# Five banks for the turned scores and one for the output in a narrow cross-attention

## The reference, cut to what matters

```python
query = (layernorm(x) @ w_q.T)                  # 128 queries, 32 heads of 16, 8 groups of 4 heads
key, value = ctx @ w_k.T, ctx @ w_v.T           # 2048 keys, 8 heads of 16, one for each group
scores = einsum('bghnd,bgsd->bghns', query, key) / 16 ** 0.5
scores = where(mask, scores, finfo.min)
attention = softmax(scores, axis=-1)
x = x + einsum('bghns,bgsd->bghnd', attention, value) @ w_out.T
```

## Time and profile before

| | us |
|---|---|
| median of 3 runs (1639.43 to 1639.99) | 1639.66 |
| profiled execution, device time | 1641.53 |
| profiled execution, span from first to last instruction | 1639.7 |
| PE (TensorE matmul) busy | 1529.1 (93%) |
| DVE (VectorE) busy | 1018.2 (62%) |
| ACT (ScalarE) busy | 874.7 (53%) |
| POOL (GpSimd) busy | 401.8 (25%) |

### The profile page before, as it was taken

How to read it: one execution, slowest core, us unless ns; L and a number is a source line. 1 busy time by engine, 2 the same in 40 slices (tenths; PEclk the granted TensorE clock), 3 DMA queues, 4 the chain that set the end, 5 groups by cost and what they waited for, 6 DMA issues and landing times. The chain is left out here.

```text
span 1639.7 us, 22771 instructions
## 1 busy us (share of the span) xinstructions
PE 1529.1 (93%) x7405; PEld 1144.4 (70%) x7405; DVE 1018.2 (62%) x2102; ACT 874.7 (53%) x1603; POOL 401.8 (25%) x349
## 2 busy tenths in 40 slices
PE   7999999999999988999888888898999999999996
PEld 5878777778784443487466665785777787778874
DVE  3036776766775883275668883663267677676773
ACT  4235665555654441255228885562366667666661
POOL 0001111101111340054327775450011011110131
PEclk9999999999999999999999999998999999999999
DMA  9431222112165007263273421745321122211130
GB/s 323 124 116 59 84 77 75 64 39 79 51 250 204 21 25 256 110 182 123 93 127 46 49 37 53 240 148 212 117 96 56 35 83 77 83 44 46 51 127 14
DMA packets 82088, 167.89 MB, mean 102 GB/s; under 512 B 6768, under 2 KB 48880, under 8 KB 72160
## 3 DMA queue, kind: packets, MB, share of 16 engines
q1 hardware_dynamic: 82016, 166.99, 32.4%
HBM read 142.07 MB, written 17.04 MB: 97 GB/s over the span
## 5 line engine op out<-in xcount | busy, mean ns | idle before, releaser
L2644 POOL TENSOR_TENSOR L2x_p_lo<-L2x_e_t,L2x_p_hi 128x512 fp32r<-128x512 f32 x96 | 122.1, 1294 | 37.7 <-ACT L2x_p_hi L2839 37.6
L736 DVE TENSOR_TENSOR L0x_k_lo<-bank,L0x_k_hi 128x512 fp32r<-128x512 f32 x128 | 85.3, 687 | 53.5 <-ACT L0x_k_hi L638 53.5
L1388 DVE TENSOR_TENSOR L3x_k_lo<-bank,L3x_k_hi 128x512 fp32r<-128x512 f32 x128 | 86.1, 688 | 52.0 <-ACT L3x_k_hi L1280 51.7
L965 POOL TENSOR_TENSOR L3x_v_lo<-L3x_v_raw,L3x_v_hi 128x512 fp32r<-128x512 f32 x32 | 40.5, 1300 | 301.2 <-ACT L3x_v_hi L1271 301.2
L361 POOL TENSOR_TENSOR L0x_v_lo<-L0x_v_raw,L0x_v_hi 128x512 fp32r<-128x512 f32 x32 | 40.5, 1305 | 295.7 <-ACT L0x_v_hi L629 295.7
L638 ACT ACTIVATE L0x_k_hi<-bank 128x512 fp32r<-128x512 f32 x128 | 74.0, 598 | 51.1 <-PE bank L511 50.5
L2893 DVE CUSTOM_DVE_ANT_0 L2x_junk<-bank,L2x_mask 128x512 f32<-128x512 f32 x128 | 86.6, 687 | 23.4 <-PE bank L2732 16.4
L1280 ACT ACTIVATE L3x_k_hi<-bank 128x512 fp32r<-128x512 f32 x128 | 74.1, 605 | 41.4 <-PE bank L1130 41.2
L1377 DVE CUSTOM_DVE_ANT_0 L3x_s<-bank,L3x_mask 128x512 f32<-128x512 f32 x128 | 80.8, 687 | 3.9 <-PE bank L1028 2.0
L725 DVE CUSTOM_DVE_ANT_0 L0x_s<-bank,L0x_mask 128x512 f32<-128x512 f32 x128 | 80.8, 687 | 3.9 <-PE bank L434 2.0
L632 ACT ACTIVATE L0x_s<-L0x_s,L0x_neg_max 128x2048 f32<-128x2048 f32 x32 | 64.3, 2008 | 30.1 <-DVE L0x_neg_max L729 30.1
(11 more groups left out here) (659 smaller groups left out, 4420.1 us busy)
## 6 DMA issues: line engine op xcount, KB each, us to landing
L0x_w_q<-in_L0x_kq SPq DMA_DIRECT2D x8, 1024.0 KB, 5.5
L0x_values<-L0x_v_raw SPq DMA_DIRECT2D x32, 256.0 KB, 2.2
L0x_w_o<-in_L0x_o SPq DMA_DIRECT2D x8, 1024.0 KB, 4.8
L0x_v_raw<-L0x_values SPq DMA_DIRECT2D x8, 1024.0 KB, 4.8
L1a_w_o<-in_L1a_o SPq DMA_DIRECT2D x8, 1024.0 KB, 6.6
L2a_w_o<-in_L2a_o SPq DMA_DIRECT2D x8, 1024.0 KB, 7.1
L3x_w_q<-in_L3x_kq SPq DMA_DIRECT2D x8, 1024.0 KB, 5.3
L3x_w_o<-in_L3x_o SPq DMA_DIRECT2D x8, 1024.0 KB, 4.7
```

The lines of the kernel that those rows point to most:

```text
L736: dve.tensor_tensor(p_lo[:, kt % 4, :], ring_bank(kt)[:], bits(p_hi[:, kt % 4, :]), ALU.subtract).then_inc(p_ready, 1)
L1388: dve.tensor_tensor(p_lo[:, kt % 4, :], ring_bank(kt)[:], bits(p_hi[:, kt % 4, :]), ALU.subtract).then_inc(p_ready, 1)
L2644: pool.tensor_tensor(p_lo[:, t % 8, :], e_of(t), bits(p_hi[:, t % 8, :]), ALU.subtract).then_inc(low_pool, 1)
```

## The change

The turned scores get a ring of five banks, 0, 1, 2, 3 and 7. The query stack no longer uses the output bank but takes a slot of this ring, between tile 13 and tile 14 of the group before; group 0's stack is in bank 6. The ring's slots are listed in the order in which TensorE fills them, and each use waits for the reader of the slot five before: the multiply out of the stack (`m_kept`), the exp, or VectorE's low half. All groups' outputs add up in bank 6, so the first weighing of a group waits for the eviction of the group before (`o_kept` of `g`, in place of `g - 1`). ScalarE evicts at `j == LAG - 1`, that is 4, in place of 6.

```diff
-        st_bank = lambda t: core.bank[t % 4]
+        ring = (0, 1, 2, 3, 7)
+        slots = [(t, stack) for t in range(NG * KT) for stack in ((False, True) if t % KT == 13 and t < NG * KT - KT
+                                                                  else (False,))]
+        slot_of = {entry: slot for slot, entry in enumerate(slots)}
+        st_bank = lambda t: core.bank[ring[slot_of[t, False] % 5]]
+        stack_bank = lambda g: core.bank[ring[slot_of[(g - 1) * KT + 13, True] % 5] if g else 6]
         s_bank = lambda n: core.bank[4 + n % 2]
-        out_bank = lambda g: core.bank[6 + g % 2]
+        out_bank = core.bank[6]
...
+                def wait_for_slot(slot):
+                    if slot >= 5:
+                        t, stack = slots[slot - 5]
+                        if stack:
+                            pe.wait_ge(m_kept, t // KT + 2)
+                        elif by_pool(t):
+                            pe.wait_ge(exp_done, t + 1)
+                        else:
+                            pe.wait_ge(low_dve, dve_count(t + 1))
+
                 def stack_queries(g):
                     pe.wait_ge(max_low, g + 1)
-                    if g >= 2:
-                        pe.wait_ge(o_kept, g - 1)
-                    pe.matmul(out_bank(g)[:], ident_r[:], q_sc[g % 2][:], start=True, stop=False)
-                    pe.matmul(out_bank(g)[:], max_rows[g % 2][:], idents[:], start=False, stop=True).then_inc(m_ready, 1)
+                    if g > 0:
+                        wait_for_slot(slot_of[(g - 1) * KT + 13, True])
+                    pe.matmul(stack_bank(g)[:], ident_r[:], q_sc[g % 2][:], start=True, stop=False)
+                    pe.matmul(stack_bank(g)[:], max_rows[g % 2][:], idents[:], start=False, stop=True).then_inc(m_ready, 1)
 
                 def turned_score(g, j):
                     t = g * KT + j
-                    if t >= 4:
-                        if by_pool(t - 4):
-                            pe.wait_ge(exp_done, t - 3)
-                        else:
-                            pe.wait_ge(low_dve, dve_count(t - 3))
+                    wait_for_slot(slot_of[t, False])
...
                     if j == 0:
                         pe.wait_ge(v_kept, g + 1)
-                        if g >= 2:
-                            pe.wait_ge(o_kept, g - 1)
+                        pe.wait_ge(o_kept, g)
...
-                    if j == LAG + 1 and g > 0:
+                    if j == LAG - 1 and g > 0:
                         keep_output(g - 1)
```

More of the change, by code:

```diff
@@ L2765, in weigh @@
                         pe.wait_ge(v_kept, g + 1)
-                        if g >= 2:
-                            pe.wait_ge(o_kept, g - 1)
+                        pe.wait_ge(o_kept, g)
                     for p in (p_hi, p_lo):
-                        mm = pe.matmul(out_bank(g)[:], v_st[g % 2][:, j * VW:j * VW + P], p[:, t % 8, :],
+                        mm = pe.matmul(out_bank[:], v_st[g % 2][:, j * VW:j * VW + P], p[:, t % 8, :],
                                        start=(j == 0 and p is p_hi), stop=(j == KT - 1 and p is p_lo))
@@ L2824, in keep_output @@
                         act.wait_ge(o_in[g % 2], 48 * (g // 2))
-                    act.activation(by_head(o_st[g % 2][:]), by_half(out_bank(g)[0:VW, :]), ACT.Copy).then_inc(o_kept, 1)
+                    act.activation(by_head(o_st[g % 2][:]), by_half(out_bank[0:VW, :]), ACT.Copy).then_inc(o_kept, 1)
                 def exponential(t):
@@ L2905, in keep_queries @@
                     dve.wait_ge(m_ready, g + 1)
-                    dve.tensor_tensor(by_half(q_st[g % 2][0:64, :]), by_head(out_bank(g)[0:64, :]), by_head(heads_sb[:]),
+                    dve.tensor_tensor(by_half(q_st[g % 2][0:64, :]), by_head(stack_bank(g)[0:64, :]), by_head(heads_sb[:]),
                                       ALU.mult).then_inc(m_kept, 1)
```

## The result

| | before | after |
|---|---|---|
| median (7 runs each) | 1643.4 (1639.43 to 1644.62) | 1630.88 (1627.7 to 1634.12) |
| ratio, 95% interval | | 0.9932 (0.9916 to 0.9948) |
| profiled execution, span | 1639.7 | 1627.6 |
| start of the first turned score to start of the last eviction | 162.29 | 151.32 |

The account below looks back on a forecast made before the run. No engine is full; engines waiting for each other, chiefly turned scores for VectorE's low half, set the 19.88 us period. Gains 8.6 + 1.5 + 1.6 = 11.7 from median 1639.66 give 1628.0 us, own range 1626 to 1630.5, wider 1623 to 1634.

Parts of the forecast that it names:

- The mechanism: Turned scores at tiles 3, 6 and 10: a fifth bank removes their waits for VectorE's low half four tiles back.
- The rival that the wait only moves on by a tile: Turned scores: the low-half wait moves one tile on and stays as long; 1639.7 us, chance 0.07.
- that of the single bank as a loss of 0.69 in each group: First weighing from group 1 on: no ring gain, seven groups each pay 0.69; 1644.5 us, chance 0.05.
- The group gain: Groups 1 to 5: period 18.16 us, 1.72 saved per group, 8.6 for the five.
- The walk: Group starting at 908.70, followed tile by tile through the engines with durations from the profile: next tile 0 at 926.86.
- 0.47 of the 0.69 is really paid: First weighing's new 0.69 us eviction stall: without it tile 7 would start at 916.32, so 0.47 is paid.
- The bound: Eviction's wait at the first weighing: at best nothing, at worst one more exp and rounding pair ahead, 1.0 us more.
- Group 0, 1.5 forecast: Group 0, with two scores in most steps and part at clock 0.50: tile 12 comes 1.5 us ahead.
- Group 6 and the last, 1.6 forecast: Group 6 reaches tile 14 about 1.65 ahead; the stretch after only starts sooner, eviction's move under 0.1: 1.6 us.
- the slower rival: First weighing of each group from 1 on: the single output bank's eviction wait makes the kernel slower; 1644.5 us, chance 0.05.
- The rival that they slip out: VectorE's value copies escape GpSimd's subtractions, tile 2's score no longer waits: 0.72 + 0.03 more per group; 1623.5 us, chance 0.14.
- One rival's sum: VectorE binds sooner than the walk says: a group saves 0.9, 7 x 0.9 = 6.2; 1633.5 us, chance 0.20.

Follow-up runs that it names:

- the kernel without the wait: Changed kernel with evictions of groups 0 to 6 reading an SBUF tile and the first weighing waiting for none: stage 150.19 us, period 18.17.
- The kernel with both moves: Changed kernel with both value copies on ScalarE and the eviction ahead of tile 3's rounding: ratio to before 0.9914, then 0.9899 when run again.
- the eviction first: Changed kernel with ScalarE's eviction put ahead of tile 3's rounding in its step of tile 4: period 18.18 us, one execution.
- The second comparison: Changed kernel unaltered, run again beside the kernel with value copies on ScalarE and earlier eviction: ratio to before 0.9943, median 1632.92 us.

## Why the prediction was right, and where it was off

**The mechanism was right.** The wait for the low half was a matter of where TensorE stands, not of how late VectorE is: one bank more moved it out of the way at tiles 3, 6 and 10, and the kernel with four banks shows that nothing else of the change did. The rival that the wait only moves on by a tile is dead. So is that of the single bank as a loss of 0.69 in each group: without the ring's gain the ratio was 0.9994 and the period the same. The clock was 1.00 from group 1 to the last in both profiles of the changed kernel.

**The group gain, 1.72 forecast, 1.55 measured.** The walk held to a tenth up to the first weighing (6.67 us after tile 0, 6.70 forecast), the eviction (5.95 against 6.05) and tile 10 (10.93 against 10.88). Two small things were missing. After the eviction's stall tile 6 came 0.54 us later, where I had 0.46: the extra time of the first step behind a stall, which I had counted for the old stalls but not for the new one. Through VectorE's queue it moved tile 11 to 12.08 (forecast 12.01). The score of tile 11 then came 0.15 after the maximum that it waits for was ready (918.00), where I had 0.06, at 12.78 (12.62), and tile 12 at 13.55 (13.41). Five groups: 7.75 against 8.6.

**"0.47 of the 0.69 is really paid" was wrong.** It is 0.16. The ring's wait at tile 7 was followed, the score's wait for the maximum two before it was not. The sum did not suffer, since it was made on the path with the stall in it; my expectation for the kernel without the wait did. The bound, "at worst one more exp and rounding pair, 1.0 more", was tested and came out as 1.01 a group.

**Group 0, 1.5 forecast, 1.84 measured: a hit by luck.** Its clock was 0.86 before and 0.92 after. The kernel with both moves has the same ring, and its group 0 takes as long as that of the changed kernel (21.95 and 21.98 us, both at a clock of 1.00). In its second execution, with a clock of 0.85, it took 23.36, only 0.74 less than the 24.10 of the kernel before at 0.86. So about 0.7 of the 1.84 is the ring's, half of what I forecast without showing the walk, and about 1.1 goes with the clock. Whether the ring helps to keep the clock up is open: where it fell in group 0, it was 0.86 in both profiles with four banks, 0.92 in six with five and 0.85 in one.

**Group 6 and the last, 1.6 forecast, 1.38 measured.** Group 6 gave 1.62. The last group took 0.24 more, where I had put the eviction's move at under 0.1. There ScalarE has no gap, so the first weighing waited 1.49 us, and tile 6 came so late that ScalarE had to wait 0.25 for it. TensorE's and ScalarE's timelines:

```profile
983.80 0.48 PE L2779 MATMUL bank<-L2x_p_hi,L2x_v_st 128*128 128x512 f32 x1 [1.49 <-ACT L2x_o_st L2835]
```
```profile
984.01 0.64 ACT L2849 ACTIVATE L2x_p_hi<-L2x_e_t 128x512 fp32r<-128x512 f32 x1
984.78 0.58 ACT L2841 ACTIVATE bank<-bank 128x512 f32<-128x512 f32 x1
```

That is the place and the mechanism of the slower rival, in the one group where ScalarE has no gap. Three kernels bear it out: with four banks this group took 20.26 us too, without the wait 20.03, and with the eviction first 20.01, as before the change.

**VectorE's copies** stayed under GpSimd's subtractions, as forecast, and cost about the same:

```profile
905.75 0.42 DVE L2924 CAST L2x_v_st<-L2x_v_hi 128x256 fp32r<-128x256 f32 x1
906.09 1.38 DVE L2924 CAST L2x_v_st<-L2x_v_lo 128x256 fp32r<-128x256 f32 x1
```
```profile
902.24 5.09 POOL L2649 TENSOR_TENSOR L2x_p_lo<-L2x_e_t,L2x_p_hi 128x512 fp32r<-128x512 f32 x4 [0.52 <-ACT L2x_p_hi L2849]
```

The second copy ends 0.14 us after the four subtractions do (907.47 and 907.33); before the change it was 0.15 (930.82 and 930.67).

The rival that they slip out did not happen. Its price per group was near when VectorE's queue was made shorter in another way: with one copy left out a group gained 0.71 (0.75 in the rival), and with both on ScalarE 0.64. What the Trainium skill says of the shared port pair (SBUF — State Buffer, "SBUF: two separate sides") agrees with these rows; that page says that ScalarE has a port of its own, and its copy beside a subtracting GpSimd took 0.43 us.

**Range and sum.** 1630.88 lies within the range of 1623 to 1634 and 0.4 above the forecast's own 1626 to 1630.5; the seven runs of the kernel before have a median 3.7 us above the one that I started from. That the ratio's 11.2 us come so near the forecast 11.7 is in part luck: the stage gave 10.97, of which about 1.1 goes with the clock in group 0, so 9.9 are the change's. The second comparison, at 0.9943, gave 9.4. The last eviction came 10.97 sooner, counted from the first turned score, where I had said 11 to 12. One rival's sum has a slip that changes nothing: 7 x 0.9 is 6.3, not 6.2.

## What to carry to other kernels

When a producer waits for a bank, ask which reader holds it longest and how many steps later the slot is wanted. If only some readers are slow, as VectorE's four tiles are here, one more slot can remove the wait with no engine made faster. A bank taken from a double buffer cost nothing here as long as its new wait fell into idle time that already existed; past that, one microsecond more was paid whole: look then at what stands in front of the eviction on its engine, and at the stage's last group, where the idle time may be missing. Follow every wait of a step when a stall is taken away, the second semaphore too: here tile 7 came 0.62 us sooner without the eviction's wait, and the score's wait left 0.14 of it at tile 8. And before a stage's gain is put down to the change, look at the clock in its windows.

## What the runs showed of the hardware

The granted clock at the edges of the stage and outside it differed between executions of one and the same kernel: 0.92 and 1.00 in group 0 of the changed kernel (0.3 us), 1.00 and 0.85 in that of the last one (1.4 us). The last group had 0.92 to 0.95 in four of the twelve profiles, all of variants with a shorter period, though the last kernel was also seen there with 1.00. A VectorE instruction beside back-to-back GpSimd subtractions could take 1.86 us in place of 0.69, or 1.38 in place of 0.27, and which of the first two it took differed between executions of the changed kernel. Seven executions of that kernel lay between 1627.7 and 1634.12 us, while its period was 18.33 us in both of its profiles.
